# Mamba scan kernel: table-load visits placed ahead of evictions, four normalisations moved, and two turned states transposed one position earlier

## The reference, cut to what matters

```
h   = layernorm(x) * (1 + ca) + sa
fwd = mamba(h);  bwd = flip(mamba(flip(h)))
x   = x + ga * (concat(fwd, bwd) @ wproj.T + bproj)
x   = x + gb * ffn(layernorm(x) * (1 + cb) + sb)

mamba(h):  u, z = split(h @ win.T)              # 1024 channels each
           u = silu(causal 4-tap convolution of u + bconv)
           dt, B, C = split(u @ wx.T)           # 32, 16, 16
           delta = softplus(dt @ wdt.T + bdt)
           for each of 16 states n, along time t:
               s[t] = exp(delta * A[n]) * s[t-1] + (delta * u) * B[n]
               y   += s[t] * C[n]
           out = ((y + u * D) * silu(z)) @ wout.T
```

## Time and profile before

| | |
|---|---|
| median of 3 runs | 7538.63 us (7533.7 to 7550.31) |
| the profiled execution | 7541.42 us, its span 7539.2 us |
| PE, DVE, ACT, POOL busy | 6812.2, 6774.4, 6182.2, 6962.0 us |
| mean granted TensorE clock | 0.975 |
| exp, L806 | 4096 times, 693 ns |
| scan, L1143 | 1281 and 1264 ns in its two largest groups |
| dBu, L691 | 2048 times, 2363 ns |

### The profile page before, as it was taken

How to read it: one execution, slowest core, us unless ns; L and a number is a source line. 1 busy time by engine, 2 the same in 40 slices (tenths; PEclk the granted TensorE clock), 3 DMA queues, 4 the chain that set the end, 5 groups by cost and what they waited for, 6 DMA issues and landing times. The chain is left out here.

```text
span 7539.2 us, 111379 instructions
## 1 busy us (share of the span) xinstructions
PE 6812.2 (90%) x32682; PEld 4023.5 (53%) x32682; DVE 6774.4 (90%) x9064; ACT 6182.2 (82%) x13081; POOL 6962.0 (92%) x3774
## 2 busy tenths in 40 slices
PE   6899988999999999999999999999989999999889
PEld 3455555555555555555555555555555555555455
DVE  2799999999999999999999999999999999999766
ACT  1788888888888888888888888888888888888745
POOL 0899999999999999999999999999999999999678
PEclk8999999999999999999999999999999999999999
DMA  7544455444444454444444544444455444444555
GB/s 255 147 137 133 132 142 150 112 138 140 138 133 129 141 151 116 133 140 137 133 131 141 150 118 131 141 138 133 128 142 151 113 135 141 138 133 129 159 185 173
DMA packets 605402, 1064.06 MB, mean 141 GB/s; under 512 B 113584, under 2 KB 221872, under 8 KB 596336
## 3 DMA queue, kind: packets, MB, share of 16 engines
q1 hardware_dynamic: 602704, 1055.81, 48.1%
q10 hardware_dynamic: 2080, 1.05, 0.0%
HBM read 926.59 MB, written 130.03 MB: 140 GB/s over the span
## 5 line engine op out<-in xcount | busy, mean ns | idle before, releaser
L691 POOL TENSOR_TENSOR dBu<-Bb,du 128x1024 f32<-128x1024 f32 x2048 | 4793.9, 2363 | 3.4 <-DMA Bb<-bc_scratch 3.3
L806 ACT ACTIVATE scans<-delta,A 128x512 f32<-128x512 f32 x4096 | 2766.5, 693 | 409.2 <-DVE hC L1159 337.5
L1143 DVE TENSOR_TENSOR_SCAN scans<-scans,state,dBu 128x512 f32<-128x512 f32 x2016 | 2540.2, 1281 | 332.5 <-ACT scans L806 332.5
L1143 DVE TENSOR_TENSOR_SCAN dBu<-scans,state,dBu 128x512 f32<-128x512 f32 x1568 | 1962.5, 1264 | 13.5 <-ACT scans L806 10.6
L1016 PE MATMUL yT<-ident,hC 128*128 128x128 f32 x9216 | 1398.0, 282 | 302.6 <-DVE hC L1159 301.1
L1159 DVE TENSOR_TENSOR hC<-scans,Cb 128x512 f32<-128x512 f32 x2304 | 1560.2, 682 | 1.1 <-PE yT L1016 1.1
L701 POOL TENSOR_TENSOR hR<-dBu,Cb 128x512 f32<-128x512 f32 x1024 | 1304.5, 1274 | 205.5 <-DVE dBu L1143 204.9
L1016 PEld LDWEIGHTS yT<-ident,hC 128*128 128x128 f32 x9216 | 1065.0, 144 | 625.5 <-DVE hC L1159 405.4
L1009 PE MATMUL bg<-u,comb 128*128 128x512 f32 x2112 | 989.4, 594 | 1.1 <-DVE u L1124 0.9
L948 PE MATMUL bg<-hT,win_u 128*128 128x512 f32 x2112 | 967.4, 598 | 0.9 <-ACT hT L728 0.9
L970 PE MATMUL bg<-hT,win_z 128*128 128x512 f32 x2048 | 963.3, 593 | 0.0
(11 more groups left out here) (161 smaller groups left out, 7891.4 us busy)
## 6 DMA issues: line engine op xcount, KB each, us to landing
comb<-pre_scratch SPq DMA_DIRECT2D x1040, 256.0 KB, 4.6
Bb<-bc_scratch SPq DMA_DIRECT2D x264, 512.0 KB, 7.0
Cb<-bc_scratch SPq DMA_DIRECT2D x264, 512.0 KB, 7.0
win_u<-in_win SPq DMA_DIRECT2D x264, 256.0 KB, 4.6
pre_scratch<-pre SPq DMA_DIRECT2D x264, 256.0 KB, 3.8
comb<-comb_scratch SPq DMA_DIRECT2D x66, 1024.0 KB, 8.6
win_z<-in_win SPq DMA_DIRECT2D x257, 256.0 KB, 2.8
part_scratch<-pre SPq DMA_DIRECT2D x132, 256.0 KB, 2.0
```

What stands on the lines that cost most here:

```text
L691: pool.tensor_tensor(dBu[:, ring(g, q)], Bb[:, 2 * q:2 * q + 2, :], du[:, j % 2, :].unsqueeze(1).broadcast_to([P, 2, T]), ALU.mult).then_i ...
L806: act.activation(place(n)[:], delta[:, j % 2, :], ACT.Exp, scale=A[:, i % 2, j * N + n:j * N + n + 1]).then_inc(dA_made, 1)
L1143: nc.vector.tensor_tensor_scan(to, place(n)[:], dBu[:, ring(g, q), k, :], state[:, c:c + 1] if i % CH_SEQ else 0.0, ALU.mult, ALU.add).the ...
```

## The change

It has three parts, all in the order of work; no arithmetic and no buffer changes.

1. At the positions of `GATED`, ACT makes its visit directly behind the second exp, ahead of the evictions and normalisations of that position.
2. `NORM_POS` goes from 50 to 54.
3. T5 and T9 stand one position earlier on PE (T1 stays), and ACT takes them one position earlier, T9 still between the two exps of its position. Inside a position a turned state now comes after every other work that starts there, where before it came ahead of U, C, O, X, K and H; and the others have a fixed order, so U comes before C, where the list's own order decided before.

```diff
-PER_TILE += [(f"T{j * N + n}", (j * NQ + n // 2 + 1,), OWN_BANK) for j in range(MT) for n in TURNED]
-FIRST = {kind: k for k, kind in enumerate("YDZT")}
-SCHEDULE = sorted(GENERAL + PER_TILE, key=lambda entry: (entry[1][0], FIRST.get(entry[0][0], len(FIRST))))
+PER_TILE += [(f"T{j * N + n}", (j * NQ + max(n // 2, 1),), OWN_BANK) for j in range(MT) for n in TURNED]
+ORDER = {kind: k for k, kind in enumerate("YDZUCOXKHT")}
+SCHEDULE = sorted(GENERAL + PER_TILE, key=lambda entry: (entry[1][0], ORDER[entry[0][0]]))
...
-NORM_POS = 50
+NORM_POS = 54
...
                         step_dA(g, i, j, 2 * q + 1)
                         keep_state(g, j, 2 * q + 1 - KEPT_BEHIND)
+                        if p in GATED:
+                            nc.scalar.preload_act_table_set(SILU)
+                            for kind, k in GATED[p]:
+                                if kind == "C":
+                                    silu_u(freed(i, f"C{k + 1}"), k, 2, 1 - s)
+                                else:
+                                    silu_z(freed(i, f"Z{k}"))
+                            nc.scalar.preload_act_table_set(EXP_LN)
...
                         for tt in range(TT):
                             if p == NORM_POS + tt:
                                 normalize(i + 2, tt, cur)
-                        if p in GATED:
-                            nc.scalar.preload_act_table_set(SILU)
...
-                            nc.scalar.preload_act_table_set(EXP_LN)
```

More of the change, by code:

```diff
@@ L104 @@
          47: (("C", 4), ("Z", 5)), 52: (("C", 6), ("Z", 6)), 63: (("Z", 7),)}
-assert all(TAKE[f"{kind}{m + (kind == 'C')}"] <= p and (kind == "C" or p // NQ == m) for p in GATED for kind, m in GATED[p])
+assert all(TAKE[f"{kind}{m + (kind == 'C')}"] < p + (kind == "Z") and (kind == "C" or p // NQ == m) for p in GATED for kind, m in GATED[p])
 assert sorted(m for p in GATED for kind, m in GATED[p] if kind == "C") == list(range(0, MT, 2))
```

## The result

The changed kernel took 7754.38 us (median of 4 runs, 7750.88 to 7766.62) against 7538.98 of the kernel before in the same comparison (7533.7 to 7550.31): a ratio of 1.0288, 95% interval 1.0272 to 1.0303. The change costs 215 us. The forecast was 7630, 90 more than before, with 7740 as the upper end of its range. The sign was right, the size was not.

The account below looks back on a forecast made before the run. No engine alone bounds it: ACT is held by PE's products, PE by banks and a DMA chain, and DVE follows the exps. Terms sum to 2.8 us a chunk, 90 in 32, giving 7630; 8-in-10 range 7470 to 7740.

Parts of the forecast that it names:

- likeliest case: Whole kernel: the forecast itself, slower by 2.8 us a chunk, 7630 us; chance 0.48.
- term 3: U3's eviction behind the visit: PE stands about 5 us at D5, mostly covered; +0.2 us a chunk, 1.9 without cover.
- Terms 1 and 2: To tile 4's start: U0's eviction, C0 and U2's eviction each 2.2 us later; +1.2 us a chunk.
- rival (c): Waits at D5 and C0 could each bring the lower clock, 1.7 us each, 3.4 a chunk: 7740 us; chance 0.20.
- Term 4: Positions 36 to 39: T9 behind U5 and ahead of its eviction makes tile 5's first scan late; +0.7 us a chunk.
- Term 5: C5 and C6: U7 ahead of C5 makes both later, and exp 10 of tile 6; +0.7, bounds -3.0 and +2.6.
- Term 6: Positions 54 to 57: the four normalisations are hidden in ACT's waits for DVE; 0 us.
- signs to look for: In the changed profile: D5 waits about 5 us, reload waits grow, ACT's waits at U1 and C6 go, DVE's exp waits shift.
- (a): Visits fill ACT's waits, DVE keeps the gain if U2's eviction is not later: faster, 7422 us; chance 0.22.

Follow-up runs that it names:

- warm_d5: The changed kernel with three extra matmuls ahead of D5, into C2's bank: 7665.59 us, ratio 1.0163.
- u3_first: The changed kernel with the visit of position 31 alone put back behind the evictions: 7632.74 us, ratio 1.0112.
- norm_only: The kernel before with only the normalisations moved, NORM_POS = 54: 7512.24 us, ratio 0.9962.
- both_undone: The changed kernel with the visit of position 31 back behind the evictions and C ahead of U: 7508.2 us, ratio 0.995.
- visits_norm: The kernel before with visits ahead of evictions everywhere but at 31, and NORM_POS = 54: 7486.1 us, ratio 0.9924.
- c_before_u: The changed kernel with C ahead of U inside a position: 7645.39 us, ratio 1.013.
- turned_only: The kernel before with only the turned states a position up and C ahead of U: 7583.9 us, ratio 1.0054.
- u7_ahead: visits_norm with U7 listed ahead of C5 at position 43: 7586.63 us, ratio 1.0063.

## Why the prediction was wrong

The prediction's likeliest case was 2.8 us a chunk. The trace has 6.5. Most of the difference, 4.1, is term 3: the cover was assumed, and the half rate behind the wait was put at nothing. By its own steps (measured values are means of chunks 2 to 29):

- **Terms 1 and 2, to the start of tile 4: +1.2 forecast, -0.5 measured.** U0's eviction ends 2.07 us later in the chunk, as forecast (2.2). C0 starts only 0.56 later and U2's eviction ends only 0.25 later. The step that failed is the DMA chain from U0 to C0, which was taken as fixed at 12.96 us, the length in the one chunk that was followed. The store of U0's rows took 5.1 us there, 3.96 in the mean (3.34 to 5.11), and takes 2.68 (2.35 to 2.98) in the changed kernel, where it is issued 1.9 us later. So it lands only 0.6 us later. The waits agree: PE's at C0 is 0.44 in the kernel before (1.70 in the chunk followed) and 1.08 in the changed one. With U2 nearly in its old place the gains at the visits stay. (Some sums take 0.65 for an eviction of U where the list of lengths has 0.75; this is 0.1 each time.)
- **Term 3, U3 behind the visit: +0.2 forecast, about 4.3 measured** (-0.53 at tile 4's first state, +3.75 at its ninth). The place, the releaser and the order of the wait were right: 3.0 us at D5 rather than 5, the copy of yT late, DVE without exps. Two things were wrong. The cover ("DVE has some 2 us in hand") did not hold, and the price without cover, 1.9, left out that D5, C2 and the sums behind the wait would take twice as long. That half of the mechanism stood in rival (c) and was put "at nothing in the sum, because a lagging PE has other slack". The reason was wrong: everything that runs at the lower rate here stands on the chain to the copy of yT, and warm_d5 prices it at 89 us.
- **Term 4, positions 36 to 39: +0.7 forecast.** From tile 4's ninth state to tile 5's first the delay grows from 3.75 to 4.43, and from 0.26 to 0.70 in u3_first. This was right.
- **Term 5, C5 and C6: +0.7 forecast, 2.0 measured.** All of the miss lies in tile 5: to the start of tile 6 the forecast has -0.45 and the trace +0.81, and from there to state 10 both have +1.2. Counted from tile 5's first scan C5 comes 4.3 us later (forecast 4.1) and C6 3.4 (forecast 2.9), and C6 takes 1.94 us instead of 1.30. DVE's last product of the tile waits 2.8 us for a buffer behind them, out of reach of any visit. What the visit could give back against that was taken as 3.00 us, DVE's wait at tile 6's start in the one chunk; its mean is 2.49. By the experiments U7 ahead of C5 costs some 101 to 109 us, 3.3 to 3.4 a chunk.
- **Term 6, the normalisations at their new places: 0 forecast, and right.** norm_only loses nothing in tile 7. The gain from leaving the old places was counted inside term 5, as 2 x 0.82 ahead of exp 10 of tile 6. Moving them alone takes DVE's wait there from 2.99 to 1.57 us and the chunk's period down by 0.96.

The store of term 1 in SP's queue of the kernel before, in the chunk followed (the load of `gain`, the store of U0's rows, the loads for C0):

```profile
3091.05 0.34 SPq L505 DMA_DIRECT2D gain<-gain_scratch  x1
3091.50 0.37 SPq L448 DMA_DIRECT2D pre_scratch<-pre  x1
...
3096.62 1.76 SPq L453 DMA_DIRECT2D comb<-pre_scratch  x4
```

and in the changed kernel:

```profile
3178.93 0.35 SPq L505 DMA_DIRECT2D gain<-gain_scratch  x1
3181.34 0.33 SPq L448 DMA_DIRECT2D pre_scratch<-pre  x1
...
3184.08 2.02 SPq L453 DMA_DIRECT2D comb<-pre_scratch  x4
```

The loads follow the store after 5.12 us here and after 2.74 there. The slower store is issued right behind other DMAs, the faster one 2.4 us behind them; whether that is the reason is not shown.

The forecast with these sizes: 2.8 - 1.7 + 4.1 + 1.3 = 6.5. The signs to look for came nearly all: the wait at D5 in each chunk, ACT's wait for U1 gone and the one for C6 halved (1.55 to 0.83), PE's wait for the reloads up to 130.1, DVE's wait at tile 3's start down from 1.96 to 0.61 and a new one of 1.09 at its state 10. Of the rivals, (a) had its condition nearly fulfilled, U2's eviction is 0.25 later and tile 4 starts 0.5 us earlier than before, and failed all the same, because D5's wait takes all of it back. (c) comes nearest with 7740, in part by luck. It had the clock right at D5 and too small (1.7 against 2.75), it was wrong at C0, where the wait stays too short to matter, and it didn't name C6, where the lower rate is now met in every chunk.

As parts of the whole: visits and normalisations -60, visit 31 ahead +122, U7 ahead of C5 +101, turned states +22 (both_undone over visits_norm). That is 185 of 215. By the periods in the table the same parts make 6.0 of 6.5 us a chunk, so what is in no part alone is 15 to 30 us. One part of the change was run in no kernel by itself, the first half of U3 ahead of C1. Between u3_first and both_undone it shows as up to 0.5 us a chunk, between the changed kernel and c_before_u as nothing. How much of the remainder is this pair, how much is parts acting together (turned_only costs 38 us, not 22) and how much is noise stays open.

## What to carry to other kernels

Put the eviction that frees a bank ahead of anything long on its engine, and price a new wait of TensorE twice: once for the wait, once for the work behind it at half rate, which at D5 was nearly three times as much. Then ask what the late work holds (a buffer, a sum, a copy), since slack on another engine doesn't help if the buffer is behind the wait. Before a delay is passed on through a wait or a DMA, take its mean and range over all chunks: one chunk is no measure of either.

## What the runs showed of the hardware

- How long PE waited doesn't by itself tell the rate behind the wait. Over chunks 2 to 29, the waits at C6 of u7_ahead and of the changed kernel (5.1 to 6.0 us) and that at D5 (2.95 to 3.20) were followed by the lower level in every chunk. At C4 of the changed kernel (0.95 to 2.61 us) it never was. At C6 of the kernel before (2.53 to 3.85 us) it was in 15 of 28 chunks; this is one of the other 13, and its window:

```profile
1453.72 1.07 PE L963 MATMUL bg<-comb,wtap 128*32 128x512 f32 x8 [3.28 <-DMA comb<-pre_scratch]
1453.70:1459.90 6.20, 6.18 (x44) 4.20 (x44) 4.34 (x8) 5.00 (x6) 6.20 (x4) 1.00 0.61 149
```

- The time at the lower level, from the clock records of the same chunks, is 7.7 us a chunk in the kernel before, 17.9 in the changed one, 10.5 in warm_d5 and 7.4 in visits_norm.
- Six throwaway matmul instructions, 2.74 us of PE's time in a gap of 3.0, made a kernel 1.1% faster.
- Behind a wait of 4.68 us the rate was no lower than behind one of 2.96: D5 took 2.07 and C2 1.94 us in both.
- One and the same store to DRAM took 3.96 us in the mean of 28 chunks from issue to landing in one kernel and 2.68 in the other, where it was issued 1.9 us later in the chunk.
